# A block with three attentions and two expert layers: the shifts' turn moved ahead of the scores into a spare PSUM bank, the early logits gathered in one turn

## The reference, cut to what matters

```python
x = L0(x)                               # attention over 256 pixels, inner width 16
x = x + L1(gn(x))                       # 8 heads of 16, all 256 pixels of an image; projection W_proj
t = tokens(x)                           # (8, 256, 128)
t = t + L2_attn(ln(t))                  # one head of 128
t = t + L2_ffn(ln(t))                   # 8 experts of 512, gelu
t = t + L3_attn(ln(t))                  # 8 heads of 16, RMS norm, rotary, causal window of 32
t = t + L3_ffn(ln(t))                   # router, best two of 8 experts of 64, a shared expert
```

```python
logits = einsum('bthc,bshc->bhts', q, k) / 4     # L3: where j <= i and j > i - 32, else -inf
attn   = softmax(logits, -1)
out    = einsum('bhts,bshc->bthc', attn, v) @ W_o
...
probs  = softmax(ln(t) @ router)                 # L3_ffn; top_k(probs, 2) weigh the experts
```

## Time and profile before

| | us |
|---|---|
| median of 3 executions (lowest, highest) | 635.94 (634.18, 640.32) |
| the profiled execution | 634.05 |
| its span, first to last instruction | 632.3 |
| TensorE busy | 570.3 (90%) |
| VectorE busy | 422.5 (67%) |
| ScalarE busy | 337.8 (53%) |
| GpSimd busy | 280.5 (44%) |
| mean granted TensorE clock | 0.967 of full speed |
| layer 1's attention, about | 65 to 165 |
| layer 3's attention, about | 465 to 563 |

### The profile page before, as it was taken

One profiled execution on the slowest core, in us unless ns is written; L12 is line 12 of the kernel. 1 busy time (PEld: TensorE's weight loads), 2 busy tenths in 40 slices (PEclk: granted clock), 3 DMA queues, 4 the chain that ended last, 5 costly groups with the idle time before them and its releaser, 6 DMA issues. The chain is left out here.

```text
span 632.3 us, 10008 instructions
## 1 busy us (share of the span) xinstructions
PE 570.3 (90%) x3288; PEld 314.2 (50%) x3288; DVE 422.5 (67%) x902; ACT 337.8 (53%) x585; POOL 280.5 (44%) x624
## 2 busy tenths in 40 slices
PE   7987998888586999999999999999799889869997
PEld 6754455554466444444444444444345566634433
DVE  2654557774365776776999799979745875564643
ACT  3542455666243786666756685668414555543221
POOL 4466003232132577778686878687421342420000
PEclk9998999999697899999999999999899999979999
DMA  6900000000000000000000000000000000000000
GB/s 164 276 3 0 1 1 2 3 1 1 2 2 1 0 1 0 0 1 2 0 1 0 1 2 1 0 1 1 0 1 2 3 2 2 3 0 2 17 18 33
DMA packets 10246, 8.63 MB, mean 14 GB/s; under 512 B 4042, under 2 KB 8148, under 8 KB 10196
## 3 DMA queue, kind: packets, MB, share of 16 engines
q1 hardware_dynamic: 10196, 8.00, 4.5%
HBM read 6.94 MB, written 1.05 MB: 13 GB/s over the span
## 5 line engine op out<-in xcount | busy, mean ns | idle before, releaser
L1584 POOL TENSOR_TENSOR h_s<-g_s 128x512 f32<-128x512 f32 x128 | 163.8, 1283 | 58.0 <-ACT g_s L1502 38.3
L1502 ACT ACTIVATE g_s<-z_s,b 128x1024 f32<-128x1024 f32 x128 | 146.5, 1149 | 63.6 <-DVE z_s L1419 38.5
L1419 DVE TENSOR_TENSOR z_s<-bank,PB 128x1024 f32<-128x1024 f32 x128 | 153.4, 1217 | 30.0 <-PE bank L1333 29.6
L1333 PE MATMUL bank<-XN_C,W 128*128 128x512 f32 x256 | 132.7, 605 | 0.3 <-PEq L1110 0.3
L1342 PE MATMUL bank<-h_s,W 128*128 128x512 f32 x256 | 130.3, 593 | 0.1
L1001 DVE TENSOR_REDUCE shiftpad<-bank 128x2 f32<-128x512 f32 (+1 forms) x128 | 72.2, 587 | 59.1 <-PE bank L815 30.4
L977 ACT ACTIVATE ET_all<-bank 128x512 f32<-128x512 f32 (+1 forms) x128 | 59.2, 514 | 74.1 <-PE bank L832 43.0
L1342 PEld LDWEIGHTS bank<-h_s,W 128*128 128x128 f32 x256 | 48.5, 190 | 62.0 <-issue 56.0
L1333 PEld LDWEIGHTS bank<-XN_C,W 128*128 128x128 f32 x256 | 47.7, 194 | 51.8 <-issue 44.4
L1057 POOL TENSOR_SCALAR var<-mv 128x2 f32<-128x2 f32 x14 | 3.3, 234 | 104.0 <-DVE mv L1041 104.0
L827 PE MATMUL bank<-Qp,Kp 17*128 17x256 f32 x256 | 36.2, 400 | 7.2 <-DVE Qp L1014 7.2
(11 more groups left out here) (331 smaller groups left out, 974.4 us busy)
## 6 DMA issues: line engine op xcount, KB each, us to landing
W<-in_L_ffn_W_dram SPq DMA_DIRECT2D x1, 2048.0 KB, 9.0
out_dram<-QK SPq DMA_DIRECT2D x4, 256.0 KB, 2.1
XN_T<-in_x_dram SPq DMA_DIRECT2D x3, 256.0 KB, 5.0
XN_T<-in_x_dram SPq DMA_DIRECT2D x2, 128.0 KB, 2.1
Wgate<-in_L_ffn_W_gate_dram SPq DMA_DIRECT2D x1, 256.0 KB, 4.4
Wup<-in_L_ffn_W_up_dram SPq DMA_DIRECT2D x1, 256.0 KB, 5.2
Wdown<-in_L_ffn_W_down_dram SPq DMA_DIRECT2D x1, 256.0 KB, 3.8
wraw<-in_L_conv_W_qkv_dram SPq DMA_DIRECT2D x1, 192.0 KB
```

Source lines behind the costliest of these rows:

```text
L1333: nc.tensor.matmul(bank[s % 4][:, :], W1[:, f // 4, f % 4 * P:(f % 4 + 1) * P], XN_C[:, g * W:(g + 1) * W], start=True, stop=True).then_in ...
L1419: nc.vector.tensor_tensor(z_s[:, s % RING, :].rearrange("p (w n) -> p w n", w=2), bank[s % 4][:, None, :].broadcast_to([P, 2, W]), PB[:, g ...
L1502: nc.scalar.activation(g_s[:, s % RING_G, :], z_s[:, s % RING, :], ACT.Gelu, bias=b1[:, f:f + 1]).then_inc(s_g, 1)
L1584: nc.gpsimd.tensor_tensor(h_s[:, s % RING, :], g_s[:, s % RING_G, 0:W], g_s[:, s % RING_G, W:2 * W], ALU.add).then_inc(s_h, 1)
```

## The change

Five things change. (1) `shift_bank(g)` sends the turned shifts of a half into bank 5 in the even steps from 10 on in layer 1 and from 12 on in layer 3, except steps 20 and 22 there (`SPARE_FROM`, `SPARE_TAKEN`); the other halves stay in bank 7. (2) Where bank 5 is used, `turn_shifts` is called ahead of the step's masks and scores; where bank 7 is, it stays behind them. The wait for bank 7's earlier readers falls away for bank 5, and one wait for the last use of bank 5 by the late groups is added before its first turn, one before step 19's transposes. (3) On VectorE the half's addition comes ahead of both maxima of its step, in every step. (4) The router's logits of images 0 to 3 all go in step 33 (eight tiles, sixteen matmul instructions as before). (5) The steps of the weights on VectorE move by one step: the first two from step 32 to 33, the next three from 34 to 35, the exponential from after step 33 to after step 34.

```diff
--- before.py
+++ after.py
@@ -663,6 +663,10 @@
             BANK = (3, 4, 5, 3) + (5,) * 5
             DRIVE = {2: 2, 3: 1}
             LAST_GROUP = GROUPS - 1
+            SPARE_FROM, SPARE_TAKEN = 10, ()
+
+            def wait_spare(self, pe):
+                self.wait_kept(pe, len(self.PARTS) - 1)
 
             def __init__(self):
                 self.s_made, self.s_kept, self.s_kept_v = local("l1_late_made"), local("l1_late_kept"), local("l1_late_v_kept")
@@ -778,6 +782,7 @@
             s_warm = local(name + "_array_driven")
 
             width = 2 * (KEYS if windowed else N)
+            late.s_sh_read = s_sh
 
             def image_at(s, lag):
 
@@ -790,6 +795,12 @@
                 return g if (s - lag) % 2 == 0 and 0 <= g < HALVES else None
 
             LAST = 4 * (IMAGES - 2) + AT_XT + 1
+
+            def shift_bank(g):
+
+                s = 2 * g + AT_MT
+                return bank[RING_S + RING_T] if s >= late.SPARE_FROM and s not in late.SPARE_TAKEN else bank[7]
+
             drive = {s: 2 for s in range(WARM)} if late is None else late.DRIVE
             with nc.Block() as block:
                 @block.tensor
@@ -852,13 +863,15 @@
                         pe.wait_ge(s_nm, (g + 1) * SLOTS)
                         if g >= 1:
                             pe.wait_ge(s_sh, g)
-                        if g >= 4:
+                        if late is not None and 2 * g + AT_MT == late.SPARE_FROM:
+                            late.wait_spare(pe)
+                        if g >= 4 and shift_bank(g) is bank[7]:
                             if g % 2 == 0:
                                 pe.wait_ge(s_oTs, g // 2 - 1)
                             else:
                                 pe.wait_ge(s_r, g // 2 - 1)
                         for t in range(NT):
-                            ins = nc.tensor.transpose(bank[7][:, t * P:(t + 1) * P],
+                            ins = nc.tensor.transpose(shift_bank(g)[:, t * P:(t + 1) * P],
                                                       shiftpad[:, g % 2, t, :, :].rearrange("p j r -> p (j r)"), ident[:, :])
                         ins.then_inc(s_MT, 1)
 
@@ -895,6 +908,9 @@
                                 ins = nc.tensor.transpose(bank[7][:, t * P:(t + 1) * P],
                                                           XN_T[:, n * N + t * P:n * N + (t + 1) * P], ident[:, :])
                             ins.then_inc(s_xT, 1)
+                        turning = half_at(s, AT_MT)
+                        if turning is not None and shift_bank(turning) is not bank[7]:
+                            turn_shifts(turning)
                         us = [u for u in (2 * s, 2 * s + 1) if u < UNITS]
                         vs = [v for v in (2 * (s - AT_T), 2 * (s - AT_T) + 1) if 0 <= v < UNITS]
                         if vs:
@@ -912,8 +928,8 @@
                             for _ in range(drive[s]):
                                 ins = nc.tensor.matmul(bank[6][:, :], Wp[:, :], XN_C[:, 0:W], start=True, stop=True)
                             ins.then_inc(s_warm, 1)
-                        if (g := half_at(s, AT_MT)) is not None:
-                            turn_shifts(g)
+                        if turning is not None and shift_bank(turning) is bank[7]:
+                            turn_shifts(turning)
                         if (n := image_at(s, AT_OT)) is not None:
                             pe.wait_ge(s_o, n + 1)
                             for t in range(NT):
@@ -941,7 +957,8 @@
                                                        start=True, stop=True)
                             ins.then_inc(s_y, 1)
                         if weights is not None:
-                            if (n := WEIGHT_LOGITS.get(s)) is not None:
+                            for n in WEIGHT_LOGITS.get(s, ()):
+                                pe.wait_ge(s_sh, HALVES)
                                 pe.wait_ge(s_done, n + 1)
                                 weights.logits(pe, n * NT, range(n * NT, (n + 1) * NT), bank[RING_S + RING_T])
                             if s in (LAST - 2, LAST - 1):
@@ -982,7 +999,7 @@
                                 act.wait_ge(s_y, n)
                             nc.scalar.copy(oT[:, :], bank[7][:, 0:N]).then_inc(s_oTs, 1)
                         if weights is not None:
-                            if s == BURSTS + 1:
+                            if s == BURSTS + 2:
                                 weights.exp(act)
                             if s in (LAST - 2, LAST - 1):
                                 weights.keep(act, s - LAST + 2, bank[RING_S + RING_T])
@@ -1005,14 +1022,13 @@
                     for s in range(LAST):
                         if late is not None and s >= 1:
                             late.dve(dve, s - 1)
-                        if s < BURSTS:
-                            highest(2 * s)
                         if (g := half_at(s, AT_MT)) is not None:
                             image, half = g // 2, g % 2
                             q = Qp[:, half, image * N:(image + 1) * N]
                             dve.wait_ge(s_MT, g + 1)
-                            nc.vector.tensor_tensor(q, bank[7][:, 0:N], q, ALU.add).then_inc(s_sh, 1)
+                            nc.vector.tensor_tensor(q, shift_bank(g)[:, 0:N], q, ALU.add).then_inc(s_sh, 1)
                         if s < BURSTS:
+                            highest(2 * s)
                             highest(2 * s + 1)
                         if s == WARM:
                             dve.wait_ge(s_warm, len(drive))
@@ -1685,8 +1701,8 @@
                 act.wait_ge(self.s_wT, i + 1)
                 nc.scalar.copy(wT[:, a:a + W], to[0:PARTS * EXPERTS, :]).then_inc(self.s_kept, 1)
 
-        WEIGHT_LOGITS = {24: 0, 25: 1, 27: 2, 31: 3}
-        WEIGHT_STEPS = {0: (0, 1), 2: (2, 3, 4), 3: (5,), 4: (6, 7), 5: (8, 9, 10, 11), 6: (12, 13, 14, 15, 16)}
+        WEIGHT_LOGITS = {33: (0, 1, 2, 3)}
+        WEIGHT_STEPS = {1: (0, 1), 3: (2, 3, 4, 5), 4: (6, 7), 5: (8, 9, 10, 11), 6: (12, 13, 14, 15, 16)}
         late_weights = ExpertWeights("l3_w_late", range(ALL // 2, ALL))
         qk3_l = sb("qk3_l", [P, TILES, 2 * P])
         qa_l = sb("qa_l", [P, TILES, 2 * P])
@@ -1703,6 +1719,11 @@
             NEWTON3_AT = {13: (0, 1), 14: (2, 3), 15: (4, 5), 16: (6, 7), 17: (8, 9, 10)}
             ADD_AT, SCALE_AT = 14, 17
             FIRST_USE = 4 * (IMAGES - PAIR)
+            SPARE_FROM, SPARE_TAKEN = 12, (20, 22)
+
+            def wait_spare(self, pe):
+                pe.wait_ge(self.s_v, TILES)
+
 
             def __init__(self):
                 (self.s_yT, self.s_r, self.s_mv, self.s_rs, self.s_xn, self.s_xT, self.s_xk, self.s_made, self.s_qk, self.s_v) = (
@@ -1738,6 +1759,8 @@
                     a = self.g * W + t * P
                     nc.tensor.matmul(to[:, 0:3 * P], XN_C[:, a:a + P], Wqkv3[:, :], start=True, stop=True).then_inc(self.s_made, 1)
                 if 0 <= (t := s - self.TURN3) < TILES:
+                    if t == 0:
+                        pe.wait_ge(self.s_sh_read, (self.TURN3 - AT_MT) // 2 + 1)
                     pe.wait_ge(self.s_qp, t + 1)
                     if t >= 1:
                         pe.wait_ge(self.s_Ts, t)
```

## The result

The changed kernel takes **648.8 us** (median of 6 runs, 644.04 to 653.21), the kernel before 635.87 (6 runs on the same chip); the ratio is 1.0188 [1.0148, 1.0228] (the bracket is a 95% interval). Forecast were 640.8, range 631 to 646: slower, as the likeliest case had it, but by 12.9 us in place of 4.9, and above the range. The profiled execution took 649.52 us around a span of 647.8, with a mean granted TensorE clock of 0.947; before it was 634.05, 632.3 and 0.967. This pair differs by 15.5 us, the medians by 12.9.

A forecast was written before the change was run, and what follows sets the result against it. TensorE's 13.0 us of waits for the add were taken to be held by the exponentials too. Layer 1 +4.7, layer 3 -1.1 and drain +2.2 gave +5.8: 639.9 on the profiled execution, 641.7 on the median; middle 640.8, range 631 to 646.

The forecast's parts named there:

- the likeliest case: The prediction's own sum, slower at 640.8 us, own range 638.5 to 642.8, chance 0.45.
- Two releasers end together: Layer 1, after even steps: exponentials hold TensorE until 114.29 anyway; removing the add gains only 0.02 us there.
- The turn ahead of the scores: Layer 1: early turn waits for the maxima, +0.54 and +0.27, gains 0.42; +0.39 per cycle, +1.95 over five.
- The holds at the start: Layer 1, steps 2, 4, 6, 8: add ahead of both maxima delays a maximum that scores need; +2.5 us together.
- the sum: All terms together: layer 1 +4.7, layer 3 -1.1, drain +2.2, making +5.8 us.
- the other reading: Scores served one after the other, not in parallel strips: a hold costs 0.2 instead of 0.56, the sum 1.0 lower.
- Layer 3: Layer 3's attention: holds +0.3, spare-bank steps +0.9 and -1.2, logits out of the steps -1.1; together -1.1 us.
- The drain: End of layer 3's attention: logits burst in step 33 +1.5, three later softmax steps +0.7; together +2.2 us.
- The first (622): Layers 1 and 3: all 13.0 us of TensorE's waits for the add vanish, giving 622 us; chance 0.10.
- The second (the turn waits for nothing): Maxima released in time, so a turn costs only its 0.27: +3.0, 638 us; chance 0.25 shared with the third.
- third (it evens out): Turns' gains and costs cancel; holds, drain and logits leave +3.9, 638.8 us; chance 0.25 shared with the second.
- The fourth (VectorE late with the values): Steps after a projection: VectorE becomes the bound, 0.5 in each of six layer 1 cycles, 643.8 us; chance 0.20.

The follow-up runs named there:

- v3: Changed kernel plus a product nothing reads behind the scores of layer 1's even steps that turn ahead; 645.55 us, ratio 1.0144.
- z1: Kernel before with the add ahead of both maxima in steps 2, 4, 6 and 8 of layer 1 alone; 638.33 us, ratio 1.0015.
- z3: Kernel before with two more driving matmuls in layer 1 (two in place of one in step 3, one in step 4); 641.71 us, ratio 1.0064.
- x1: Kernel before with the add ahead of both maxima in all steps, the turn staying behind the scores; 655.36 us, ratio 1.0293.
- z4: x1 plus one product nothing reads, behind the turn in even steps 10 to 30 of layer 1; 640.86 us, ratio 1.0054.
- y1: Kernel before with a finished image's transposes moved to the free half of the spare bank; 637.47 us, ratio 1.0009.
- v2: y1 plus the filler product of v1; 633.75 us, ratio 0.9972.
- v1: Kernel before plus a 256-column product nothing reads, behind the turn in even steps 10 to 30 of layer 1; 636.21 us, ratio 1.0009.
- v4: Kernel before with a 512-column filler product in every second even step of layer 1; 636.26 us, ratio 1.0003.
- z2: Kernel before with only layer 1's early turns from step 10; old VectorE order in bank 7 steps, layer 3 and logits as before; 644.77 us, ratio 1.0101.
- x2: Changed kernel with the old order (first maximum, add, second maximum) in the steps that keep bank 7; 645.89 us, ratio 1.0164.
- y2: x2 with layer 1's early turns starting at step 16 instead of 10; 641.38 us, ratio 1.0080.
- x4: Changed kernel with two more driving matmuls in steps 3 and 4 of layer 1; 651.40 us, ratio 1.0234.

## Why the prediction was wrong in size

**Two releasers end together: right.** With the add gone from the path, the next step starts at 125.80, held by the exponentials, and the idle part of the gap is 0.76 in place of 0.81.

**The turn ahead of the scores: right.** The cycle was to grow by 0.39 to 10.53; it grew by 0.27 to 10.44. The turn waits for the maxima (123.53, 0.06 after their end), as computed.

**The holds at the start: right.** Forecast 0.45, 0.2 and 0.56 for steps 2 to 6, measured in v3 0.48, 0.28 and 0.58. For step 8 with the first early turn behind it the forecast was 1.32: from the turn of step 8 to the first scores of step 10 v3 takes 96.21 - 91.33 = 4.88 us and the kernel before 91.79 - 88.22 = 3.57, 1.31 more. Together 2.65 against the sum's 2.5. In z1 steps 2, 6 and 8 cost 0.49, 0.58 and 0.59; with 0.28 for step 4 that is 1.9, and the median moved by 1.8. That a single late strip holds the step, and not only its own quarter, is borne out by 0.58 where the other reading had 0.2.

**Layer 3: right.** -1.1 forecast, -1.0 measured to the end of step 32.

**The drain: right at full clock.** +2.2 forecast, +3.1 measured, of which 0.96 is the low clock at 566 to 570 us (above). The rest is near its terms: the burst takes 1.70 from its start to the next masks and not 1.48. From the image's transposes (569.23, before 554.95) to the projection of the last image (572.83, before 557.84) it is 3.60 us against 2.89, 0.71 more, where the softmax's three steps were put at 0.7.

**The failed step is the sum itself: every duration was taken from rows at a granted clock of 1.00, as the earlier trace rows shows it, and the sum had no term for the clock and no rival either.** I read the 1.00 as a property of the stage. The same stage stood at 0.50 for 17 us and 3 more in the changed kernel, and for 20 us in the kernel before with only its start shifted (z3). In the profiled pair the clock makes 9.0 us in layer 1 and 1.0 in the drain; without them the 15.5 is 5.5, where the sum said 5.8. At an equal clock the sum is about right in other executions, too: those with a mean clock of 0.952 took 640.2 to 640.7 us before (17 of them) and 645.57 after (one), 5 apart; with 0.946 they took 643.5 to 643.7 before (4), and with 0.947 648.1 to 649.6 after (5), 4 to 6 apart; with 0.955 to 0.957 they took 636.4 to 638.9 before and 644.0 and 644.1 after, 5 to 8 apart; the sum said 5.8. The clock's share of the 12.9 is what is left, 5 to 8 us, an estimate, since the mean clock of the whole span is a coarse measure.

**Rivals.** The first (622) fell with the exponentials. The second (the turn waits for nothing) and third (it evens out) were near in their terms, too, but the turn does wait. The fourth (VectorE late with the values) doesn't show: the products of values of layer 1 wait 1.2 us in one place for the exponentials, as before, and the cycle has no 0.5 in it. None of the four had the mechanism that decided.

**Shown, and open.** Shown is that the surplus over the sum is time at the low level of the clock, 10 of the profiled pair's 15.5 us, and that one product in each wait brings the clock back in one order: 14.5 us (x1, z4). In a second (y1, v2) it is worth 3.7 by the medians, at the edge of the noise; in the kernel before it does nothing (v1, v4). In the changed kernel its 3 to 4 us (v3) are not clear of the noise. Not shown is what makes the clock fall. The early turns are suspect: z2, x2 and y2 have stretches at half speed behind them and mean clocks of 0.949, 0.949 and 0.955, and the holds alone leave it at 0.959 (z1). Against them as the sole cause stand two things. The changed kernel falls at 77.9 us, in steps whose code is z1's, 23 us ahead of its first early turn, and 7.4 of the 9.0 us lie there; TensorE was busy there as in the kernel before, 9.39 of 10 us, and 4.48 against 4.19 of the next 5. And z3 falls for 20 us with no early turn at all. The rival that is left is that of x4 and z3: whether the clock falls hangs on how the stretches of work and waiting lie in time, which any change of the start shifts. Nothing here separates the two. For steps 4 to 8 the only filler tried was x4's driving in steps 3 and 4, and the fall came later instead.

## What to carry to other kernels

Where a profile shows TensorE at full clock and nearly full, give the forecast a term for the clock: a change of order, or of the start alone, can bring stretches at half speed that cost more than its waits. In the trace of the changed kernel, read the granted clock per stretch before looking for anything else, and compare executions at an equal mean clock. When a move takes work out of a wait that something else imposes anyway, nothing is won, and the wait is now bare: leave the work there, or put a product that nothing reads in its place and see whether the clock comes back. And when two releasers end within 0.02 us, taking one away is worth next to nothing, here 0.03.

## What the runs showed of the hardware

- One product of 128x256 in each of eleven waits of TensorE took 14.5 us off a kernel of 655 us (x1 655.36, z4 640.86) at an unchanged cycle, with the granted clock from 140 to 160 us at 1.00 in place of 0.68. A lower busy share did not mean a lower clock: from 110 to 140 us TensorE was busy 28.0 of 30 us in x1, whose clock fell next, and 26.3 in the kernel before, whose clock did not.
- A fall can come late: x1 ran seven intervals of two steps, 5.3 us each with the same waits, at 1.00 before its long one; x4, with two more matmuls at the start, fell at 100 us and not at 78, and the kernel before with the same two at 106 (z3). The same code has executions at different mean clocks: the kernel before ran from 0.946 (643.5 to 643.7 us) to 0.967 (633.6 to 634.5).
- At the low level two 128x512 fp32 matmuls took 2.08 us in place of 1.13, and sixteen products of values 1.91 in place of 1.06, while the busy time of TensorE looked the same: 5.00 of 5 us.
- Of the sixteen products of a step in four strips of the array, one held back by some 0.56 us (an estimate, from the prediction's count on the earlier trace rows) delays the whole step by 0.58 (z1, interval from step 6: 6.67 against 6.09).
